# Linear attention between two FP4 feed-forwards: scores in tiles of 32 feature rows, and issued ahead of the numerator

## The chip, the core and the metric

The kernel runs on one core of a Trainium2 chip. The metric is the device time of one execution in microseconds, the median of the runs shown. A core has TensorE (matmuls; PE in the profile, PEld for its weight loads), VectorE (DVE), ScalarE (ACT), GpSimd (POOL) and SyncE (SP), which here only issues DMAs. Each engine goes through its own instructions in order; semaphores tie the engines together. Matmul results go to PSUM, eight banks of 2 KB for each of 128 partitions.

## The reference

The input x is 16 x 1024 tokens of 256 features. Three layers, each after a layernorm and with a residual:

```python
x = x + 0.5 * ffn(layernorm(x))
x = x + attention(layernorm(x))
x = x + 0.5 * ffn(layernorm(x))
# attention, 16 heads of 16 features:
q = (elu(q) + 1 + 1e-4) / 4 ; k = elu(k) + 1 + 1e-4
num[l] = q[l] @ cumsum_l(k[l] v[l]^T) ; den[l] = q[l] . cumsum_l(k[l]) + 1e-4
out = layernorm((num / den) @ Wout.T + bout) * gamma + beta
```

The feed-forward (256 to 704 to 256) rounds activations and weights to FP4 values by blocks of 16.

## The kernel before

The 16384 tokens are 128 tiles of 128 tokens; x stays in SBUF (`x_sb`). Three stages follow each other: the first feed-forward over all tiles (to about 760 us), attention (to about 1490), the second feed-forward. At the borders their steps alternate. Each stage is a software pipeline. Each engine has a step function (`sync_step`, `vector_step`, ...) that is called for i = 0, 1, 2, ... (in hardware loops of 4 steps in attention) and works on several tiles, i + 4 to i - 4; the order of the calls to it written out in the function is the order of the engine's queue, and nothing reorders it. Buffers alternate by the parity of the tile (`pair`).

Attention step i on TensorE, in order: q and k projection of tile i + 1 (L1260), transpose of k(i) (L1267), v projection of i + 1 (L1276); ten waits; numerator of i - 1, a part from the masked scores (64 matmuls, L1300) and a part from the running state (16 matmuls, L1305); scores of i (32 matmuls, L1313); the state's increments from tile i (L1328); output projection of i - 2 (L1337, L1340). A tile is split into two halves of 64 tokens. The state of the earlier tiles and halves is added through q_feat; inside a half the scores k.q are masked causally. A matmul over feature rows would add up several heads, so heads are kept apart by zeros: k is written twice (`k_eo`: rows of even heads, rows of odd heads), and q twice (`q_rows`: every other pair of heads), so that a 64 x 64 tile holds two pairs and gives 128 columns.

VectorE in step i: statistics of x(i + 4) (L1052) and of the output (L1058), the causal mask on the scores of i - 1 (L1062), residual of i - 4 (L1072), aggregates (L1074, L1076), the state `before` (L1082), gamma (L1086), the denominators of i - 1 (L1090), features of i + 1 (L1094), the reciprocal (L1097), o(i - 1) (L1103), the state's two parts (L1108, L1115).

ScalarE: high half of o(i - 2) (L1187), q_feat (L1192), q_rows (two activations, L1194), then for i + 1 the feature ramp (L1206), v (L1213), exp (L1215); k in token rows (L1223), v's own half (two, L1229), x normalized (L1235) and its high half (L1239).

GpSimd: k's even part (L1143) and odd part (L1144), low half of o(i - 2) (L1148), the state `mid` (L1155), low half of x(i + 2) (L1159), rstd (L1170, L1172), shift (L1176), beta (L1178).

SyncE: two copies of v(i + 1) to the other half (L1027), the transpose of o(i - 1) (L1033), the transpose of x(i + 3) (L1039). They wait for `v_nat`, `o_split` and `x_split`.

PSUM banks in attention: q/k 0, transpose of k and first state part 1, scores 2 and 3, v and second state part 4, numerator 5 and 6, output 7. The scores have one buffer, the numerator too.

Of the kernel before, what the change touches and what calls it, by code (L numbers as in the profile page):

```python
# [28 lines left out]
BF16 = mybir.dt.bfloat16  # L29
# [7 lines left out]
P = 128  # L37
D = 256
# [301 lines left out]
def prepare_ffn(nc, sem, scratch, wg, wu, wd, wgu_hi, wgu_lo, wd_hi, wd_lo, unscale, ident, ident16, minus_half, eps, minus_one, offsets):  # L340
# [6 lines left out]
    with ExitStack() as scope:  # L347
# [155 lines left out]
        def tensor_gate_up(pe):  # L503
            for s, (w, n, src, _) in enumerate(sets):
# [8 lines left out]
                for j, a in enumerate(src):  # L513
                    last = nc.tensor.transpose(ps[:, s % 3, j * P:(j + 1) * P], a, ident16[:])
# [27 lines left out]
        def from_bank(s):  # L542
            return ps[:, s % 3, 0:len(sets[s][2]) * P].rearrange("p (t c j) -> p c t j", c=DC, j=SUB)
# [46 lines left out]
def ffn(nc, S, T, at, N, half, x_sb, x_t, out_t, wgu_hi, wgu_lo, wd_hi, wd_lo, unscale, minus_half, eps, minus_one, offsets,  # L590
# [4 lines left out]
    with ExitStack() as scope:  # L595
# [198 lines left out]
        def scalar_step(act, i, par):  # L794
# [52 lines left out]
        def tensor_step(pe, i, par):  # L847
            tg, td = i, i - 4
            if valid(tg, N):

                if half == 1 and isinstance(tg, int) and tg == 0:
                    pe.wait_ge(T["kv_first"], N)
                    pe.wait_ge(T["o_ready"], N)
# [10 lines left out]
            if valid(td, N):  # L864
# [14 lines left out]
             "q_feat", "q_rows", "v_done", "v_nat", "v_own", "v_eo_even", "v_eo_odd", "kT_done", "k_nat", "scores_done", "masked", "kv_done", "kv_first", "kv_second",  # L879
# [8 lines left out]
class Constants:  # L888
# [11 lines left out]
    of_pair: object  # L900
    of_pair_eps: object
# [8 lines left out]
def attention_constants(sbuf, N):  # L910
    def sb(name, shape, dt=F32):
# [4 lines left out]
                     sb("of_pair", [P, 2]), sb("of_pair_eps", [P, 2]), sb("eps2", [P, 2]), sb("own", [P, DC, PAIRS]), sb("ones3", [P, P], BF16), sb("bout3", [P, D], BF16),  # L916
# [4 lines left out]
               "k_eo": (15104, 17152), "scores": 19200, "v_nat": (23296, 24384), "v_eo": (25472, 27648), "q_feat": (29824, 30848), "q_rows": (31872, 33920),  # L921
# [5 lines left out]
def attention(nc, S, at, N, x_sb, A, ident, minus_half, eps, F, attn_added, set_up):  # L927
    unscale, o_scale, one, rows, causal, diag, even, odd, of_pair, of_pair_eps, eps2, own, ones3, bout3, feat_eps, keep = (
        A.unscale, A.o_scale, A.one, A.rows, A.causal, A.diag, A.even, A.odd, A.of_pair, A.of_pair_eps, A.eps2, A.own, A.ones3, A.bout3, A.feat_eps, A.keep)
    with ExitStack() as scope:  # L930
# [19 lines left out]
        q_rows = pair("q_rows", [P, DC, 2, P])  # L950
# [5 lines left out]
        scores = sb("scores", [P, 2, DC, 2, 2, SUB])  # L956
# [38 lines left out]
        num = ps_num[:, :, 0:WIDE].rearrange("p g (h w) -> p g h w", w=VW)  # L995
# [558 lines left out]
```

## Time and profile before

| | |
|---|---|
| median of 3 runs | 2227.42 us (2226.64 to 2227.62) |
| profiled execution, its own time | 2225.92 us |
| its span, first to last instruction | 2224.2 us |
| mean granted TensorE clock | 0.994 of full speed |
| TensorE, VectorE, ScalarE, GpSimd busy | 95%, 93%, 86%, 85% |
| HBM traffic over the span | 17 GB/s |

The span is that of one execution recorded by the profiler. Busy leaves out waiting, branches and issuing of DMAs. Matmuls overlap, so a group of short ones is better read by the distance of their starts than by their durations. "issue" as the cause of idle time means that the profile shows no other instruction that the engine waited for; SPq is SyncE's queue, and a row of it is the time that issuing took, not the transfer's.

### The profile page before, as it was taken

Reading aid. Unit: us, or ns where it says so; the run is one execution under the profiler, and the core shown is the slowest. Engines: PE = TensorE matmul, PEld = TensorE weight load, DVE = VectorE, ACT = ScalarE, POOL = GpSimd, SP = SyncE. Lnnn points to the kernel's source line nnn. Section 1 sums busy time; section 2 is a strip of 40 time slices with the busy share of each in tenths; the row PEclk is TensorE's granted clock in tenths of the full one; section 3 lists DMA queues with packets and bytes.
Section 4 is the critical chain, followed back from the end, with each engine's and each line's share of the span. In section 5 each row is a group of like instructions: output and inputs, shape, how many; then the busy total and the mean of one; then the engine's idle time right before and its main releaser. Section 6 shows DMA issues by size and latency. Waiting matters only on the chain.

```text
span 2224.2 us, 91039 instructions
## 1 busy us (share of the span) xinstructions
PE 2124.0 (95%) x30384; PEld 1496.2 (67%) x30384; DVE 2066.5 (93%) x5231; ACT 1915.0 (86%) x4136; POOL 1897.5 (85%) x3002
## 2 busy tenths in 40 slices
PE   3899999999999899999999999979999999999998
PEld 1566666666666688888888888855666665666565
DVE  7999999999999689999999999978999999999997
ACT  7888888888888789999999999978888888888885
POOL 6899999999999678888888888868989999989996
PEclk9999999999999999999999999999999999999999
DMA  4765555555556432222222222224655555555555
GB/s 104 128 121 115 116 113 112 115 116 114 114 112 109 75 56 60 60 59 59 59 59 58 60 59 58 60 47 79 114 112 112 112 112 112 112 112 113 112 117 117
DMA packets 719856, 208.74 MB, mean 94 GB/s; under 512 B 666400, under 2 KB 719520, under 8 KB 719776
## 3 DMA queue, kind: packets, MB, share of 16 engines
q1 hardware_dynamic: 719776, 207.76, 46.5%
q8 instruction: 40, 0.66, 0.1%
q14 instruction: 40, 0.33, 0.1%
HBM read 20.38 MB, written 16.78 MB: 17 GB/s over the span
## 4 chain that ended last, share of the span: by engine, by line
DVE 41%; PE 25%; issue 13%; POOL 12%; DMA 4%; DVEq 2%; SPq 2%; ACT 1%; POOLq 0%; ACTq 0%
DVE ffn_y L748 10%; DVE ffn_per_block L717 9%; DVE ffn_hx L710 7%; PE ffn_ps_gu L860 6%; PE attn_ps_qk L1260 5%; DVE ffn_q L744 3%; PE ffn_ps_down L872 3%; DMA attn_xT<-attn_x_hl 3%; POOL ffn_h_hl L791 3%; POOL ffn_h_hl L790 3%; PE attn_ps_num L1300 3%; PE attn_ps_v_second L1276 2%; PE attn_ps_sc L1313 2%; DVE ffn_scale L723 2%; SPq L1033 2%
## 5 line engine op out<-in xcount | busy, mean ns | idle before, releaser
L860 PE MATMUL ffn_ps_gu<-wgu_hi,ffn_xT 128*128 128x512 f16 (+1 forms) x3072 | 739.0, 363 | 16.2 <-DVE ffn_hx L710 7.5
L860 PEld LDWEIGHTS ffn_ps_gu<-wgu_hi,ffn_xT 128*128 128x128 f16 x3072 | 300.9, 98 | 302.6 <-issue 21.7
L806 ACT ACTIVATE ffn_quarter<-ffn_y,offsets 128x960 int16<-128x960 f32 (+2 forms) x264 | 282.6, 1071 | 185.2 <-DVE ffn_y L748 185.2
L860 PE MATMUL ffn_ps_gu<-wgu_lo,ffn_xT 128*128 128x512 f16 (+1 forms) x1536 | 431.5, 363 | 0.0
L872 PE MATMUL ffn_ps_down<-wd_hi,ffn_hT 128*128 128x256 f16 x2816 | 349.9, 273 | 18.8 <-DVE x_sb L737 12.7
L790 POOL TENSOR_TENSOR ffn_h_hl<-ffn_q,ffn_h_scale_hi 128x704 f16<-128x704 f16 x256 | 352.2, 1376 | 12.5 <-DVE ffn_h_scale_lo L754 8.5
L791 POOL TENSOR_TENSOR ffn_h_hl<-ffn_q,ffn_h_scale_lo 128x704 f16<-128x704 f16 x256 | 354.0, 1383 | 0.0
L872 PEld LDWEIGHTS ffn_ps_down<-wd_hi,ffn_hT 128*128 128x128 f16 x2816 | 265.1, 98 | 99.0 <-issue 35.5
L717 DVE TENSOR_REDUCE ffn_per_block<-ffn_hx 128x60 f32<-128x960 f32 (+2 forms) x264 | 298.4, 1130 | 21.3
L748 DVE TENSOR_TENSOR ffn_y<-ffn_hx,ffn_per_block 128x960 f32<-128x960 f32 (+2 forms) x264 | 294.8, 1117 | 0.0
L842 ACT ACTIVATE ffn_odd<-ffn_quarter,offsets 128x960 f16<-128x960 int16 (+2 forms) x264 | 278.7, 1056 | 10.8 <-POOL ffn_shift L783 10.8
L710 DVE SCALAR_TENSOR_TENSOR ffn_hx<-ffn_ps_gu,unscale,ffn_silu 128x704 f32<-128x704 f32 x256 | 243.3, 950 | 13.8 <-issue 9.5
L860 PEld LDWEIGHTS ffn_ps_gu<-wgu_lo,ffn_xT 128*128 128x128 f16 x1536 | 150.8, 98 | 155.9 <-issue 3.4
L801 ACT ACTIVATE ffn_silu<-ffn_ps_gu,unscale 128x704 f32<-128x704 f32 x256 | 212.0, 828 | 17.8 <-PE ffn_ps_gu L860 17.7
L781 POOL TENSOR_TENSOR ffn_x_hl<-ffn_q,ffn_x_scale_hi 128x256 f16<-128x256 f16 x256 | 157.8, 616 | 73.5 <-POOL ffn_rstd L773 37.4
L872 PE MATMUL ffn_ps_down<-wd_lo,ffn_hT 128*128 128x256 f16 x1536 | 210.2, 273 | 0.0
L1260 PE MATMUL attn_ps_qk<-attn_xT,attn_w_hi 128*128 128x128 f16 x2048 | 179.9, 220 | 11.1 <-DMA attn_xT<-attn_x_hl 5.6
L773 POOL TENSOR_TENSOR ffn_rstd<-ffn_rstd,minus_half 128x1 f32<-128x1 f32 x256 | 167.4, 654 | 20.0
L785 POOL TENSOR_TENSOR ffn_x_hl<-ffn_q,ffn_x_scale_lo 128x256 f16<-128x256 f16 x256 | 159.9, 624 | 20.0
L872 PEld LDWEIGHTS ffn_ps_down<-wd_lo,ffn_hT 128*128 128x128 f16 x1536 | 150.6, 98 | 17.7
L1260 PEld LDWEIGHTS attn_ps_qk<-attn_xT,attn_w_hi 128*128 128x128 f16 x2048 | 135.7, 98 | 30.9 <-DMA attn_xT<-attn_x_hl 29.4
L1062 DVE TENSOR_TENSOR attn_scores<-attn_ps_sc,attn_causal 128x1024 f32<-128x1024 f32 x128 | 154.3, 1206 | 0.0
(184 smaller groups left out, 5177.6 us busy)
## 6 DMA issues: line engine op xcount, KB each, us to landing
x_sb<-in_L_attn_x SPq DMA_DIRECT2D x128, 128.0 KB, 2.4
out<-x_sb SPq DMA_DIRECT2D x128, 128.0 KB, 2.1
attn_v_eo<-attn_v_nat SPq DMA_DIRECT2D x256, 34.0 KB, 1.8
ffn_xT<-ffn_x_hl SPq DMA_TRANSPOSE x256, 2.4
ffn_hT<-ffn_h_hl SPq DMA_TRANSPOSE x256, 3.5
attn_xT<-attn_x_hl SPq DMA_TRANSPOSE x128, 2.4
attn_oT<-attn_o_hl SPq DMA_TRANSPOSE x128, 2.5
x_sb<-in_L_ffn_w_gate SPq DMA_DIRECT2D x2, 352.0 KB, 5.2
```

The costliest lines, as they stand in the source:

```text
L710: nc.vector.scalar_tensor_tensor(hx[par][:, 0:INNER], ps_gu[par][:, INNER:2 * INNER], unscale[:, 1:2], silu[:], ALU.mult, ALU.mult).then_i ...
L717: nc.vector.tensor_reduce(amax[:, blocks_in(front)], blocks(hx[par][:, front]), AXX, ALU.max, apply_absolute_value=True).then_inc(S["amax" ...
L748: nc.vector.tensor_tensor(blocks(y[:, front]), blocks(hx[par][:, front]), over_block(inv[:, at], at.stop - at.start), ALU.mult).then_inc(S ...
L773: nc.gpsimd.tensor_tensor(rstd[oth][:], rstd[oth][:], minus_half[:, 0:1], ALU.pow).then_inc(S["rstd"], 1)
L790: nc.gpsimd.tensor_tensor(blocks(h_hl[par][:, 0:INNER]), blocks(q[par][:, 0:INNER]), over_block(h_scale_hi[par][:], HB), ALU.mult)
L791: nc.gpsimd.tensor_tensor(blocks(h_hl[par][:, INNER:]), blocks(q[par][:, 0:INNER]), over_block(h_scale_lo[par][:], HB), ALU.mult).then_inc ...
L801: nc.scalar.activation(silu[:], ps_gu[par][:, 0:INNER], ACT.Silu, scale=unscale[:, 0:1]).then_inc(S["silu"], 1)
L806: nc.scalar.activation(quarter[:, back], y[:, back], ACT.Identity, bias=offsets[:, 0:1], scale=4.0 / HALF_MIN).then_inc(S["quarter"], 1)
L842: nc.scalar.activation(odd[:, back], quarter[:, back], ACT.Identity, bias=offsets[:, 1:2], scale=HALF_MIN / 4.0).then_inc(S["odd"], 1)
L860: last = nc.tensor.matmul(ps_gu[par][:, a:b], xT[par][:, c, :], w[:, k, a:b], start=(n == 0), stop=(n == len(terms) - 1))
L872: last = nc.tensor.matmul(ps_down[:, 0:D], hT[par][:, c, :], w[:, c, :], start=(n == 0), stop=(n == len(terms) - 1))
L1260: last = nc.tensor.matmul(ps_qk[:, col, :], w[:, col, k], aT, start=(n == 0), stop=(n == len(terms) - 1))
```

## The change

- Scores: instead of 32 matmuls with 64 feature rows and 128 columns (both pairs of heads through `q_rows`), 64 matmuls with 32 feature rows (one pair) and 64 columns, straight from `q_feat`. `q_rows` is gone, with its constants. Each of the four row groups writes to a bank of its own.
- PSUM: `ps_sc_num` has four banks, 2 to 5; the scores lie in columns 0 to 255 of each, the numerator in columns 256 to 391 of the last two. v and the second state part move to bank 6. The first feed-forward's `per_block` moves between its two `ps_gu`, and the set-up's transposes move by one bank.
- k's odd part moves from GpSimd to ScalarE, behind q_feat, as an activation with scale `odd` and bias `odd * 1e-4`.
- Order: on TensorE the scores of i now come after the v projection and ahead of the numerator of i - 1, with waits of their own (both parts of k, q_feat, the mask of i - 1, o of i - 2); the waits of the numerator stand behind them. On VectorE the mask of tile i moves from step i + 1 to the end of step i, and waits also for the numerator of i - 1.
- At the border to the second feed-forward its first gate/up matmuls wait for the last mask, and the second ones for the last o.

The diff, cut to this (left out: the same shift of a bank in the set-up's transposes, the lists of semaphores and constants, and `k_odd`/`q_rows` in their declarations):

```diff
@@ -626,8 +626,8 @@
         hT = pair("hT", [P, HLC, P], F16)
 
         if half == 0:
-            ps_gu = [psum(f"ps_gu{j}", [P, 3 * 512]) for j in range(2)]
-            per_block = psum("per_block", [P, 2, 256])
+            ps_gu_even, per_block, ps_gu_odd = psum("ps_gu0", [P, 3 * 512]), psum("per_block", [P, 2, 256]), psum("ps_gu1", [P, 3 * 512])
+            ps_gu = [ps_gu_even, ps_gu_odd]
             ps_down = psum("ps_down", [P, 512])
         else:
             per_block = psum("per_block", [P, 2, 256])
...
@@ -831,6 +831,7 @@
 
                 if half == 1 and isinstance(tn, int) and tn < 2:
                     act.wait_ge(T["v_done"], N)
+                    act.wait_ge(T["k_even"], N + tn - 1)
                     act.wait_ge(T["k_odd"], N + tn - 1)
                 ready(act, "shift", tn)
                 round_freed(act, "y", i + 1, 2)
...
@@ -850,6 +851,8 @@
 
                 if half == 1 and isinstance(tg, int) and tg == 0:
                     pe.wait_ge(T["kv_first"], N)
+                    pe.wait_ge(T["masked"], N)
+                if half == 1 and isinstance(tg, int) and tg == 1:
                     pe.wait_ge(T["o_ready"], N)
                 turned(pe, "xT", tg, par)
                 freed(pe, "silu", tg, 2)
...
@@ -967,9 +968,8 @@
 
         ps_qk = psum("ps_qk", [P, 2 * DC, P])
         ps_kT_first = psum("ps_kT_first", [P, 512])
-        ps_sc = psum("ps_sc", [P, 2, DC, 2, 2, SUB])
+        ps_sc_num = psum("ps_sc_num", [P, PAIRS, 512])
         ps_v_second = psum("ps_v_second", [P, 512])
-        ps_num = psum("ps_num", [P, 2, 512])
         ps_z = psum("ps_z", [P, 512])
 
         def ready(eng, name, t, k=1, per=1):
...
@@ -992,7 +992,8 @@
 
         ps_kT, ps_v = ps_kT_first[:, 0:D], ps_v_second[:, 0:D]
         WIDE = DC * PAIRS * VW
-        num = ps_num[:, :, 0:WIDE].rearrange("p g (h w) -> p g h w", w=VW)
+        ps_sc = ps_sc_num[:, :, 0:DC * P].rearrange("p r (c s q) -> p r c s q", c=DC, s=2)
+        num = ps_sc_num[:, 2:4, DC * P:DC * P + WIDE].rearrange("p g (h w) -> p g h w", w=VW)
 
         def half_state(s):
             return (ps_kT_first, ps_v_second)[s][:, D:D + WIDE]
...
@@ -1056,11 +1057,6 @@
                 if not (isinstance(tz, int) and tz < 2):
                     dve.wait_ge(S["rstd"], tz + 5)
                 nc.vector.bn_stats(z_bn6[:], ps_z[:, 0:D]).then_inc(S["z_sums"], 1)
-            if valid(tm, N):
-
-                ready(dve, "scores_done", tm)
-                nc.vector.tensor_tensor(scores[:].rearrange("p g c s j q -> p (g c s j) q"), ps_sc[:].rearrange("p g c s j q -> p (g c s j) q"),
-                                        causal[:].unsqueeze(1).to_broadcast([P, 4 * PAIRS, SUB]), ALU.mult).then_inc(S["masked"], 1)
             if valid(tz, N):
                 ready(dve, "z_sums", tz)
             if valid(ts, N):
...
@@ -1113,6 +1109,13 @@
                 if isinstance(i, int) and i == 0:
                     last_turned(dve, "hT_even")
                 nc.vector.tensor_tensor(by_head(first[:]), half_state(0).rearrange("p (h w) -> p h w", w=VW), own_head(), ALU.mult).then_inc(S["kv_first"], 1)
+            if valid(i, N):
+
+                ready(dve, "scores_done", i)
+                if valid(tm, N):
+                    ready(dve, "num_done", tm)
+                nc.vector.tensor_tensor(scores[:].rearrange("p r c s q -> p r (c s) q"), ps_sc.rearrange("p r c s q -> p r (c s) q"),
+                                        causal[:].unsqueeze(1).unsqueeze(1).to_broadcast([P, PAIRS, 2 * DC, SUB]), ALU.mult).then_inc(S["masked"], 1)
 
 
         def gpsimd_step(pool, i, par):
...
@@ -1141,7 +1144,6 @@
                 pool.sem_inc(S["turn"], 1)
                 k = expo[par][:, DC:2 * DC, :].rearrange("p c (s t) -> p c s t", s=2)
                 nc.gpsimd.tensor_scalar(k_eo[par][:, :, :, 0, :], k, FEAT_EPS, even[:], ALU.add, ALU.mult).then_inc(S["k_even"], 1)
-                nc.gpsimd.tensor_scalar(k_eo[par][:, :, :, 1, :], k, FEAT_EPS, odd[:], ALU.add, ALU.mult).then_inc(S["k_odd"], 1)
             if valid(to, N):
 
                 ready(pool, "o_hi", to)
...
@@ -1190,9 +1192,7 @@
                 ready(act, "feat", i)
                 freed(act, "num_done", i, 2)
                 nc.scalar.activation(q_feat[par][:], expo[par][:, 0:DC, :], ACT.Identity, bias=feat_eps[:]).then_inc(S["q_feat"], 1)
-                for j in range(2):
-                    last = nc.scalar.activation(q_rows[par][:, :, j, :], expo[par][:, 0:DC, :], ACT.Identity, bias=of_pair_eps[:, j:j + 1], scale=of_pair[:, j:j + 1])
-                last.then_inc(S["q_rows"], 1)
+                nc.scalar.activation(k_eo[par][:, :, :, 1, :], expo[par][:, DC:2 * DC, :].rearrange("p c (s t) -> p c s t", s=2), ACT.Identity, bias=odd_eps[:], scale=odd[:]).then_inc(S["k_odd"], 1)
             if valid(tf, N):
 
                 if isinstance(tf, int) and tf == 0:
...
@@ -1200,7 +1200,7 @@
                     act.wait_ge(F["q"], N + X_AHEAD)
                 ready(act, "qk_done", tf)
                 freed(act, "q_feat", tf, 2)
-                freed(act, "q_rows", tf, 2)
+                freed(act, "k_even", tf, 2)
                 freed(act, "k_odd", tf, 2)
                 freed(act, "kT_done", tf, 2)
                 nc.scalar.activation(expo[oth][:], ps_qk[:], ACT.Relu, bias=one[:], scale=unscale[:, 1:2]).then_inc(S["relu"], 1)
...
@@ -1275,10 +1275,25 @@
                 for n, (aT, w, k) in enumerate(terms):
                     last = nc.tensor.matmul(ps_v.rearrange("p (t m) -> p t m", t=DC), aT, w[:, 2 * DC:QT, k], start=(n == 0), stop=(n == len(terms) - 1))
                 last.then_inc(S["v_done"], 1)
+            if valid(i, N):
+
+                if isinstance(i, int) and i == 0:
+                    pe.wait_ge(F["y"], N + X_AHEAD)
+                ready(pe, "k_even", i)
+                ready(pe, "k_odd", i)
+                ready(pe, "q_feat", i)
+                freed(pe, "masked", i, 1)
+                freed(pe, "o_ready", tn, 1)
+                pe.sem_inc(S["turn"], 1)
+                for c in range(DC):
+                    for s in range(2):
+                        for a in range(2):
+                            for r in range(PAIRS):
+                                rows_of = slice(r * 2 * E, (r + 1) * 2 * E)
+                                last = nc.tensor.matmul(ps_sc[half(a), r, c, s], k_eo[par][rows_of, c, s, a], q_feat[par][rows_of, c, half(s)], start=True, stop=True)
+                last.then_inc(S["scores_done"], 1)
             if valid(tn, N):
 
-                if isinstance(tn, int) and tn == 0:
-                    pe.wait_ge(F["y"], N + X_AHEAD)
                 ready(pe, "mid", tn)
                 if not (isinstance(tn, int) and tn == 0):
                     pe.wait_ge(S["before"], tn)
...
@@ -1287,17 +1302,12 @@
                 ready(pe, "v_own", tn)
                 ready(pe, "masked", tn)
                 freed(pe, "o_ready", tn, 1)
-            if valid(i, N):
-                ready(pe, "k_odd", i)
-                ready(pe, "q_rows", i)
-                freed(pe, "masked", i, 1)
-            if valid(tn, N):
                 for c in range(DC):
                     for r in range(PAIRS):
                         for u in range(4):
                             s, m = u // 2, u % 2
                             h = c * PAIRS + r % 2 * 2
-                            nc.tensor.matmul(num[quarter(u), r // 2, h:h + 2, :], scores[:, r // 2, c, s, r % 2, quarter(m)], v_eo[oth][:, s, :, c * PAIRS + r, :],
+                            nc.tensor.matmul(num[quarter(u), r // 2, h:h + 2, :], scores[:, r, c, s, quarter(m)], v_eo[oth][:, s, :, c * PAIRS + r, :],
                                              start=(c == 0 and r % 2 == 0), stop=False, skip_group_check=True)
                 for c in range(DC):
                     for s, st in enumerate((before, mid)):
...
@@ -1305,13 +1315,6 @@
                             last = nc.tensor.matmul(num[half(s), g, c * PAIRS:(c + 1) * PAIRS, :], q_feat[oth][half(g), c, half(s)], st[oth][half(g), c],
                                                     start=False, stop=True, skip_group_check=True)
                 last.then_inc(S["num_done"], 1)
-            if valid(i, N):
-                for c in range(DC):
-                    for s in range(2):
-                        for a in range(2):
-                            for g in range(2):
-                                last = nc.tensor.matmul(ps_sc[half(a), g, c, s], k_eo[par][half(g), c, s, a], q_rows[par][half(g), c, :, half(s)], start=True, stop=True)
-                last.then_inc(S["scores_done"], 1)
             if valid(i, N):
 
                 ready(pe, "k_nat", i)
...
@@ -1464,9 +1465,7 @@
         last.then_inc(top_ready, 1)
         dve.wait_ge(even_ready, 1)
         nc.vector.tensor_scalar(A.odd[:], A.even[:], -1.0, 1.0, ALU.mult, ALU.add).then_inc(done, 1)
-        dve.wait_ge(pair_ready, 1)
-        then(dve, nc.vector.tensor_tensor(of_pair[:], in_pair[:, 0:2], in_pair[:, 2:4], ALU.add))
-        nc.vector.tensor_scalar(A.of_pair_eps[:], of_pair[:], FEAT_EPS, None, ALU.mult).then_inc(done, 1)
+        nc.vector.tensor_scalar(A.odd_eps[:], A.even[:], -FEAT_EPS, FEAT_EPS, ALU.mult, ALU.add).then_inc(done, 1)
 
     def tops_made(pe):
         pe.wait_ge(top_ready, 1)
```

## Rows read from the trace of the kernel before

**Rows 1.** The page's busy time per engine, share of the span, instructions.
```profile
PE 2124.0 (95%) x30384; PEld 1496.2 (67%) x30384; DVE 2066.5 (93%) x5231; ACT 1915.0 (86%) x4136; POOL 1897.5 (85%) x3002
```

**Rows 2.** Windows, attention stage: length, busy time by engine, clock, DMA share, GB/s.
```profile
760.00:1460.00 700.00, 680.22 (x20567) 599.20 (x20561) 650.31 (x1714) 651.65 (x1479) 562.20 (x1105) 1.00 0.30 59
```

**Rows 3.** Source line L1090, 820 to 1440 us: duration, first and last start, waits.
```profile
L1090 DVE TENSOR_SCALAR attn_den<-attn_ps_num,attn_o_scale x110: 233/234/236, 824.7 to 1436.0; 128x16 f32<-128x16 f32 x110
...
  PE attn_ps_num L1305: 25.7, 92
```

**Rows 4.** Waits, 900 to 1300 us: who waited for whom, total, times, longest.
```profile
PEld attn_ps_num L1300 <- issue: 22.2, 71, 0.5
...
PEld attn_ps_qk L1260 <- DMA attn_xT<-attn_x_hl: 11.3, 39, 0.4
...
PE attn_ps_num L1300 <- issue: 5.6, 26, 0.2
```

**Rows 5.** Timeline 1116 to 1122 us: start, length, instruction, idle before it.
```profile
1116.29 0.23 DVE L1090 TENSOR_SCALAR attn_den<-attn_ps_num,attn_o_scale 128x16 f32<-128x16 f32 x1 [0.37 <-PE attn_ps_num L1305]
...
1117.38 0.42 DVE L1103 TENSOR_TENSOR attn_o<-attn_ps_num,attn_rden 128x256 f32<-128x256 f32 x1
...
1118.19 0.42 DVE L1052 BATCH_NORM_STATS2 attn_bn<-x_sb 128x6 f32 x1
...
1116.35 0.64 ACT L1229 ACTIVATE attn_v_eo<-attn_v_nat 64x136 f32<-64x136 f32 x2 [0.23 <-PE attn_ps_num L1305]
...
1117.98 0.40 ACT L1187 ACTIVATE attn_o_hl<-attn_o 128x256 f16<-128x256 f32 x1
...
1118.25 0.48 POOL L1144 TENSOR_SCALAR attn_k_eo<-attn_expo,attn_odd 128x256 f32<-128x256 f32 x1
1118.81 0.67 POOL L1148 TENSOR_TENSOR attn_o_hl<-attn_o,attn_o_hl 128x256 f16<-128x256 f32 x1
...
1119.71 1.19 SPq L1033 DMA_TRANSPOSE attn_oT<-attn_o_hl  x1
1121.16 1.19 SPq L1039 DMA_TRANSPOSE attn_xT<-attn_x_hl  x1
```

**Rows 6.** The same view, 1125 to 1133 us: the way from the transpose to the denominators.
```profile
1125.97 0.76 PE L1300 MATMUL attn_ps_num<-attn_v_eo,attn_scores 128*32 128x34 f32 x64
...
1126.66 0.28 PE L1305 MATMUL attn_ps_num<-attn_before,attn_q_feat 64*64 64x68 f32 x2
...
1126.80 1.19 SPq L1039 DMA_TRANSPOSE attn_xT<-attn_x_hl  x1
...
1126.95 1.05 PE L1313 MATMUL attn_ps_sc<-attn_q_rows,attn_k_eo 64*64 64x128 f32 x32
...
1129.29 0.40 PE L1260 MATMUL attn_ps_qk<-attn_xT,attn_w_hi 128*128 128x128 f16 x4
...
1131.62 0.90 PE L1300 MATMUL attn_ps_num<-attn_v_eo,attn_scores 128*32 128x34 f32 x64
1132.44 0.28 PE L1305 MATMUL attn_ps_num<-attn_before,attn_q_feat 64*64 64x68 f32 x2
...
1132.98 0.23 DVE L1090 TENSOR_SCALAR attn_den<-attn_ps_num,attn_o_scale 128x16 f32<-128x16 f32 x1 [0.34 <-PE attn_ps_num L1305]
```

**Rows 7.** Groups by line and shape, 900 to 1300 us: busy, mean ns, idle before.
```profile
L1062 DVE TENSOR_TENSOR attn_scores<-attn_ps_sc,attn_causal 128x1024 f32<-128x1024 f32 x72 | 86.8, 1206 | 0.0
...
L1194 ACT ACTIVATE attn_q_rows<-attn_expo,attn_of_pair_eps,attn_of_pair 128x256 f32<-128x256 f32 x144 | 77.6, 586 | 0.0
...
L1313 PE MATMUL attn_ps_sc<-attn_q_rows,attn_k_eo 64*64 64x128 f32 x2272 | 75.1, 269 | 0.0
...
L1300 PE MATMUL attn_ps_num<-attn_v_eo,attn_scores 128*32 128x34 f32 x4544 | 58.5, 198 | 5.7 <-issue 5.6
...
L1192 ACT ACTIVATE attn_q_feat<-attn_expo,attn_feat_eps 128x256 f32<-128x256 f32 x72 | 35.5, 493 | 0.0
...
L1144 POOL TENSOR_SCALAR attn_k_eo<-attn_expo,attn_odd 128x256 f32<-128x256 f32 x71 | 34.0, 478 | 6.6
```

More of the change, by code:

```diff
@@ L513, in tensor_gate_up @@
                 for j, a in enumerate(src):
-                    last = nc.tensor.transpose(ps[:, s % 3, j * P:(j + 1) * P], a, ident16[:])
+                    last = nc.tensor.transpose(ps[:, 1 + s % 3, j * P:(j + 1) * P], a, ident16[:])
                 last.then_inc(set_turned, 1)
@@ L878 @@
 ATTN_SEMS = ("sums", "stats", "var", "rstd", "shift", "xn", "x_hi", "x_split", "turn", "xT_even", "xT_odd", "qk_done", "relu", "exp", "feat", "k_even", "k_odd",
-             "q_feat", "q_rows", "v_done", "v_nat", "v_own", "v_eo_even", "v_eo_odd", "kT_done", "k_nat", "scores_done", "masked", "kv_done", "kv_first", "kv_second",
+             "q_feat", "v_done", "v_nat", "v_own", "v_eo_even", "v_eo_odd", "kT_done", "k_nat", "scores_done", "masked", "kv_done", "kv_first", "kv_second",
              "mid", "before", "num_done", "den", "rden", "o_ready", "o_hi", "o_split", "oT_even", "oT_odd", "proj_done",
@@ L915, in attention_constants @@
                      sb("rows", [P, 3, D]), sb("causal", [P, SUB]), sb("diag", [P, DC, 2 * PAIRS]), sb("even", [P, 1]), sb("odd", [P, 1]),
-                     sb("of_pair", [P, 2]), sb("of_pair_eps", [P, 2]), sb("eps2", [P, 2]), sb("own", [P, DC, PAIRS]), sb("ones3", [P, P], BF16), sb("bout3", [P, D], BF16),
+                     sb("odd_eps", [P, 1]), sb("eps2", [P, 2]), sb("own", [P, DC, PAIRS]), sb("ones3", [P, P], BF16), sb("bout3", [P, D], BF16),
                      sb("feat_eps", [P, 1]), sb("keep", [P, N]))
 ATTN_PLACES = {"o": 8352, "oT": (1024, 2048), "o_hl": (9376, 4096), "mid": (5632, 6176), "before": (6720, 7264), "first": 7808, "second": 11264, "k_nat": 12352, "zg": 13376,
-               "k_eo": (15104, 17152), "scores": 19200, "v_nat": (23296, 24384), "v_eo": (25472, 27648), "q_feat": (29824, 30848), "q_rows": (31872, 33920),
+               "k_eo": (15104, 17152), "scores": 19200, "v_nat": (23296, 24384), "v_eo": (25472, 27648), "q_feat": (29824, 30848),
                "expo": (35968, 38016), "xT": (40064, 41088), "x_hl": (42112, 43136), "xn": 44160,
@@ L927, in attention @@
 def attention(nc, S, at, N, x_sb, A, ident, minus_half, eps, F, attn_added, set_up):
-    unscale, o_scale, one, rows, causal, diag, even, odd, of_pair, of_pair_eps, eps2, own, ones3, bout3, feat_eps, keep = (
-        A.unscale, A.o_scale, A.one, A.rows, A.causal, A.diag, A.even, A.odd, A.of_pair, A.of_pair_eps, A.eps2, A.own, A.ones3, A.bout3, A.feat_eps, A.keep)
+    unscale, o_scale, one, rows, causal, diag, even, odd, odd_eps, eps2, own, ones3, bout3, feat_eps, keep = (
+        A.unscale, A.o_scale, A.one, A.rows, A.causal, A.diag, A.even, A.odd, A.odd_eps, A.eps2, A.own, A.ones3, A.bout3, A.feat_eps, A.keep)
     with ExitStack() as scope:
@@ L955, in attention @@
         v_eo = pair("v_eo", [P, 2, 2, HEADS // 2, VW])
[L956 removed]
+        scores = sb("scores", [P, PAIRS, DC, 2, SUB])
         first, second = sb("first", [P, DC, PAIRS, VW]), sb("second", [P, DC, PAIRS, VW])
```

12 lines of the change are left out of this document (4 added, 8 removed).

## The prediction, made before the changed kernel was run

> **What bounds the kernel now.** I read the page's busy shares first, then the stage that the change touches, then the waits inside it, then single steps in order of time. Over the span TensorE and VectorE are busy 95% and 93% [rows 1], which names no bound. In the attention stage TensorE, VectorE and ScalarE stand at 97%, 93% and 93% and GpSimd at 80%, at full granted clock [rows 2]. L1090 (the denominators, once a step) starts 110 times between 824.7 and 1436.0 us [rows 3]: (1436.0 - 824.7) / 109 = 5.608 us a step. That is the number the change must move.
>
> No engine is full, so I look for loops: chains that come back to the same instruction some steps later and so set the step. VectorE waits for the numerator on TensorE before L1090 in 92 of 110 steps, 25.7 us in all. TensorE waits for the transposed x (DMA) ahead of the q/k projection in 39 of 71 steps, 11.3 us [rows 3, 4]. Both point to one way round: numerator(k) on TensorE, denominators and o(k) on VectorE, the high half of o on ScalarE (L1187), the low half on GpSimd (L1148), SyncE's transpose of o (L1033), then SyncE's transpose of x(k+4) behind it (L1039), the q/k projection(k+4) and, later in that same TensorE step, numerator(k+2). From k to k+2: two steps.
>
> Its first part in the trace [rows 5]: L1090 at 1116.29, o_hi ends at 1118.38, but o_lo starts only at 1118.81 since GpSimd was still on k's odd part until 1118.73; transpose of o at 1119.71, of x at 1121.16. Its second part [rows 6]: transpose of x at 1126.80, q/k projection at 1129.29 (2.49 later), numerator at 1131.62 (2.33), its second half L1305 at 1132.44 (0.82; in another step 1125.97 to 1126.66, 0.69), L1090 at 1132.98 (0.54). So from projection to denominators 2.33 + 0.75 + 0.54 = 3.62, and the way round is (1121.16 - 1116.29) + 2.49 + 3.62 = 10.98 over two steps, 5.49 a step. That is 0.12 under 5.608. The rest belongs to a three-step variant, in which GpSimd reaches o_lo late for its own reasons (rstd, shift, beta, k's two parts): the three steps from 1116.29 to 1132.98 are 16.69, 5.56 each.
>
> **The change, part by part.**
>
> *ScalarE* loses the two q_rows copies (2 x 586 ns, back to back 1.08) and gains one 128x256 activation like L1192, 493 ns [rows 7]: 0.6 to 0.7 us less a step. They stand behind L1187 in its order, so they never delayed o_hi of their step; what they delayed was the next L1229. That one also waits for the numerator: at 1116.35, released by the numerator like L1090, it starts 0.06 after it, and the chain to o_hi's end is 1118.38 - 1116.29 = 2.09 [rows 5]. I use 2.09, the case in which ScalarE is not late.
>
> *GpSimd* loses L1144, 478 ns [rows 7] and with its gap 1118.81 - 1118.25 = 0.56 [rows 5]. That is the stall that goes. What is late next is o_hi: o_lo can't start before 2.09 plus a hand-over. The trace has no such hand-over in the open; the nearest are numerator to ScalarE, 0.06, and o_lo's end (1119.48) to SyncE, 0.23 [rows 5]. I take 0.15. So o_lo starts 2.24 after L1090 instead of 2.52, a gain of 0.28, not 0.56. New first part: 2.24 + 0.67 + 0.23 to the transpose of o, + 1.45 to the transpose of x (SyncE spends 1.19 on the first) = 4.59, + 2.49 = 7.08.
>
> *TensorE, scores.* 32 matmuls of 64x64, 128 columns, become 64 of 32 rows, 64 columns. The old ones start 26.7 ns apart at best (1132.73 on; 32 take 0.87 with the change of shape) [rows 6]. The new ones are as many as L1300's, whose 64 take 0.69 to 0.82 including the hand-over to L1305, some 11 to 13 ns each. Bounds: if eight small ones run where four large ones ran, each costs 26.7 / 4 = 6.7 ns, 0.43 in all; if still only four run at a time, 26.7 / 2 = 13.3 ns, 0.85. I take 0.75, nearest to L1300. On TensorE's own account this is a gain of about 0.1. The Trainium skill (TensorEngine Tiling, Available Configurations) lists 32x64 as eight independent tiles; by that the 0.43 would hold and my forecast would fall by 0.16 a step, but the trace's L1300 doesn't reach such a pace.
>
> *TensorE, order.* This is the part that costs. Before, the scores of step i came behind numerator(i-1), while VectorE, ScalarE, GpSimd and SyncE were already on the way back; they were off the loop. Now they stand between the v projection and the numerator, so all of their 0.75 is added between projection and denominators. In front of the scores: waits for k_even, k_odd, q_feat, masked, o_ready and a semaphore increment, fewer than the ten that stood ahead of the numerator. Behind them: seven waits ahead of the numerator, now right after 64 short matmuls, where TensorE has no backlog to hide them. Bounds: 0, and the weight load's 22.2 / 71 = 0.31 of idle "issue" ahead of L1300 [rows 4]; TensorE itself idled only 5.6 / 71 = 0.08 there. I take 0.10. New second part: 3.62 + 0.75 + 0.10 = 4.47.
>
> What comes behind the numerator (state matmuls, out projection) follows it directly now. It needs k_nat and the transpose of o; no row shows how much they have to spare. I take them as in time, since ScalarE is relieved and the transpose of o is issued 4.59 - 1.45 = 3.14 after L1090 and lands in the 2.49 of a transpose, 5.63, while the projection comes a step and some tenths later.
>
> *VectorE.* The masking, 1206 ns for 1024 elements [rows 7], stays the same size and moves from behind the two bn_stats to behind L1115. That makes a one-step loop: masked(i), scores(i+1), numerator(i), L1090, ..., L1115, masked(i+1). L1115 ends its turn at 1118.19, 1.90 after L1090 [rows 5]; + 1.21, a hand-over 0.15 to 0.3, + 0.85, + 0.75 + 0.54 = 5.40 to 5.55. It is under the two-step loop, so masked isn't what TensorE waits for, but it isn't far away.
>
> *Shared banks.* Scores and numerator share two banks, in different columns; masked(i) waits for numerator(i-1), scores(i) for o(i-2). In program order both are long done. Nothing.
>
> *Set-up and the feed-forward stages:* a few tiny set-up operations go, the banks of the first feed-forward are renumbered, the last masking comes some time earlier. I cost them at nothing, cover being the loads at the start; bound 1 to 2 us either way.
>
> **The sum.** Two-step loop (7.08 + 4.47) / 2 = 5.775 a step. Three-step loop 16.69 - 0.56 + 0.85 = 16.98, 5.66 a step, not the bound. One-step loop at most 5.55. So the step goes from 5.608 to 5.775, +0.167. It counts for 109 full steps and, at about half, for the 18 that run beside feed-forward steps: 118 x 0.167 = +19.7. The profiled execution took 2225.9 us for a span of 2224.2; its own sum is 2245.6, and the median of the runs shown is 1.5 above it, so 2246 to 2247. I say 2246.
>
> Own range of this case: shortest 7.00 + 3.56 + 0.43, 5.50, where the other loops hold the step at about 5.55 to 5.6, no change; longest 7.16 + 3.69 + 0.85 + 0.31 = 12.01, 6.00 a step, +0.40 x 118 = +47, 2273.
>
> **Rivals.**
>
> *A. The relief wins: faster.* Mechanism: place GpSimd and ScalarE between L1090 and the transpose of o. For it: three engines stand at 93% or more, and a three-step loop through GpSimd is as tight as the trace gets; if that way back, not TensorE's stretch, sets the step, it loses 0.56 on GpSimd and 0.68 on ScalarE against 0.85 added: 16.69 - 1.24 + 0.85 = 16.30, 5.43 a step, -0.17 x 118 = -20, 2206. It decides once o_hi's end lies more than 0.5 earlier than 2.09 after L1090. Against it: q_rows stand behind o_hi, and ScalarE then waits for the numerator anyway.
>
> *B. It nets out.* Scores at the pace of eight tiles and waits hidden: 5.6 a step, 2223 to 2232.
>
> *C. The small score matmuls are no cheaper each than the large ones* (26.7 ns, 64 of them 1.71). Then the second part is 3.62 + 1.71 + 0.10 = 5.43, (7.08 + 5.43) / 2 = 6.25 a step, +76, 2302. Against it: L1300's 64 matmuls go at 11 to 13 ns each. The Trainium skill (TensorE: Matmul & The Clock Gate, "Wait — 56ns, not 53.3ns?") says that starts never come closer than about 25 ns however small the matmul; by that rule this case would be the result, but the same row contradicts it.
>
> **Chances.** Forecast 0.64, A 0.18, B 0.10, C 0.08. The range 2220 to 2276 leaves out nearly all of A below (0.12) and C above. The likeliest case's own range is 2228 to 2273. A measurement of this kernel tells a change from none at about 0.2%, 4.5 us: slower 0.68 (nearly all of the forecast, C), same 0.13 (B and the forecast's low end), faster 0.19 (A).
>
> **What would show it.** In the trace after: L1090's step near 5.78 in the same stretch; TensorE busy share falling by some 3 points, with nearly every step idle ahead of the q/k projection, put down to the transpose of x; score matmuls taking 0.7 to 0.8 from first start to the numerator's first; projection to denominators 4.4 to 4.6 instead of 3.6; o_lo starting right behind o_hi, 2.2 to 2.3 after L1090, with GpSimd idle ahead of it; ScalarE's busy share down to some 80% (5.22 busy of 5.608 now, less 0.66, over 5.775). Wrong it would be if TensorE doesn't wait for x at all (then A), or if it waits for masked ahead of the scores (then the one-step loop is longer than I made it), or if the scores take 1.5 or more (C).

## The result and the profile after

The changed kernel takes 2257.6 us (2256.1 to 2260.1), beside 2227.0 for the kernel before: ratio 1.014, interval 1.012 to 1.016. It is slower, by 30.6 us; the forecast was 19 slower, 2246, inside the range but too low. The profiled execution took 2260.1 us for a span of 2258.4.

The attention stage in windows (columns as in [rows 2]):

```profile
760.00:1460.00 700.00, 671.74 (x23729) 577.98 (x23724) 597.25 (x1661) 579.30 (x1311) 482.85 (x950) 1.00 0.27 57
```

The denominators' line, now L1086, in the stretch of [rows 3]:

```profile
L1086 DVE TENSOR_SCALAR attn_den<-attn_ps_sc_num,attn_o_scale x107: 232/234/236, 823.9 to 1435.1; 128x16 f32<-128x16 f32 x107
...
  PE attn_ps_sc_num L1315: 60.6, 107
```

The same line over the whole run:

```profile
L1086 DVE TENSOR_SCALAR attn_den<-attn_ps_sc_num,attn_o_scale x128: 226/234/236, 767.2 to 1524.0; 128x16 f32<-128x16 f32 x128
```

A step takes (1435.1 - 823.9) / 106 = 5.766 us against 5.608: +0.158, and VectorE now waits for the numerator in every step (92 of 110 in [rows 3]). On 109 steps that is +17.2. But from the first to the last denominators it is 756.8 us against 723.9 (the same line of the kernel before starts at 767.3 first and at 1491.2 last), +32.9. So 15.7 us were lost in the 18 steps at the borders, where attention alternates with a feed-forward. The two profiled executions are 34.2 us apart, so all but 1.3 us lies in attention. Relieved engines gave nothing back: ScalarE went from 652 to 579 busy and GpSimd from 562 to 483, in 700 us. VectorE, which lost no work, fell from 650 to 597 all the same: there are fewer steps in the stretch, and its residual takes 485 ns instead of 782 (means from 900 to 1300 us); no run tests why.

The waits, 900 to 1300 us (who waited for whom, total us, times, longest):

```profile
ACT attn_v_eo L1229 <- PE attn_ps_sc_num L1315: 49.4, 69, 0.8
...
DVE attn_den L1086 <- PE attn_ps_sc_num L1315: 38.3, 69, 0.8
POOL attn_o_hl L1150 <- ACT attn_o_hl L1189: 35.1, 70, 0.6
...
PEld attn_ps_qk L1260 <- DMA attn_xT<-attn_x_hl: 16.6, 36, 0.5
...
PE attn_ps_qk L1260 <- DMA attn_xT<-attn_x_hl: 5.7, 28, 0.3
```

The engines wait for one another along the way round: ScalarE and VectorE for the numerator, GpSimd for o's high half, TensorE's loads for the transpose of x. One turn of the loop in the timeline (start, length, instruction, idle before it):

```profile
1112.16 0.23 DVE L1086 TENSOR_SCALAR attn_den<-attn_ps_sc_num,attn_o_scale 128x16 f32<-128x16 f32 x1 [0.73 <-PE attn_ps_sc_num L1315]
...
1113.92 0.40 ACT L1189 ACTIVATE attn_o_hl<-attn_o 128x256 f16<-128x256 f32 x1
...
1114.41 0.68 POOL L1150 TENSOR_TENSOR attn_o_hl<-attn_o,attn_o_hl 128x256 f16<-128x256 f32 x1 [0.64 <-ACT attn_o_hl L1189]
...
1115.24 1.19 SPq L1034 DMA_TRANSPOSE attn_oT<-attn_o_hl  x1
1116.70 1.19 SPq L1040 DMA_TRANSPOSE attn_xT<-attn_x_hl  x1
...
1119.10 0.40 PE L1260 MATMUL attn_ps_qk<-attn_xT,attn_w_hi 128*128 128x128 f16 x4 [0.17 <-DMA attn_xT<-attn_x_hl]
...
1121.42 0.91 PE L1293 MATMUL attn_ps_sc_num<-attn_q_feat,attn_k_eo 32*64 32x64 f32 x64
1122.42 0.76 PE L1310 MATMUL attn_ps_sc_num<-attn_v_eo,attn_scores 128*32 128x34 f32 x64
...
1123.64 0.23 DVE L1086 TENSOR_SCALAR attn_den<-attn_ps_sc_num,attn_o_scale 128x16 f32<-128x16 f32 x1 [0.67 <-PE attn_ps_sc_num L1315]
```

First part 1119.10 - 1112.16 = 6.94, second 1123.64 - 1119.10 = 4.54, together 11.48 for two steps, 5.74 (means from 1000 us on: 6.99 and 4.55). The step alternates between some 5.6 and 5.9, and the wait for x comes about once in the two steps.

### The profile page after: what moved, and what is told of

It is laid out like the page before. It is cut to its first block and busy times, and to the rows that moved or that the text cites. A ratio compares the mean times of both kernels' runs of the same rounds, so it can differ in the third digit from the quotient of the medians.

```text
span 2258.4 us, 99286 instructions
## 1 busy us (share of the span) xinstructions
PE 2144.9 (95%) x34480; PEld 1498.4 (66%) x34480; DVE 2029.6 (90%) x5229; ACT 1861.4 (82%) x4008; POOL 1832.7 (81%) x2874
## 5 line engine op out<-in xcount | busy, mean ns | idle before, releaser
L1229 ACT ACTIVATE attn_v_eo<-attn_v_nat 64x136 f32<-64x136 f32 x256 | 80.5, 315 | 104.8 <-PE attn_ps_sc_num L1315 103.3
L875 PEld LDWEIGHTS ffn_ps_down<-wd_lo,ffn_hT 128*128 128x128 f16 x1536 | 150.6, 98 | 17.7
```

The source lines that it names most:

```text
L875: last = nc.tensor.matmul(ps_down[:, 0:D], hT[par][:, c, :], w[:, c, :], start=(n == 0), stop=(n == len(terms) - 1))
```

## The borders

In the straight-line code there, TensorE stops in the middle of blocks that hold no wait. An example (timeline, TensorE):

```profile
1483.11 0.61 PE L1310 MATMUL attn_ps_sc_num<-attn_v_eo,attn_scores 128*32 128x34 f32 x47
1485.75 0.34 PE L1310 MATMUL attn_ps_sc_num<-attn_v_eo,attn_scores 128*32 128x34 f32 x17 [2.04 <-issue]
```

47 of 64 matmuls, 2.04 us of nothing, then the other 17. In the stretches 730 to 860 and 1400 to 1530 us I count stops of TensorE of 0.8 us or more that end by "issue" in attention's own blocks: 2 in the kernel before (1.85, 0.95; 2.8 together), 9 in the changed one (1.54, 1.09, 1.75, 2.20, 1.85, 2.04, 2.14, 2.13, 2.06; 16.8 together). From 830 to 1440 us, inside the hardware loop, there is none. The DMA queue for instructions, from the page of the changed kernel (packets, MB); it was 40 packets and 0.66 MB before:

```profile
q8 instruction: 44, 0.72, 0.1%
```

That is four packets of 16 KB more; between 900 and 1300 us that queue moves nothing. The times of its packets in the traces tie the stops to it. In each of the nine stops of the changed kernel TensorE goes on 1.31 to 1.51 us after the last such packet has landed. For the stop shown, the packet starts at 1483.50 and lands at 1484.44, and TensorE goes on at 1485.75. In the two stops of the kernel before it is 1.35 and 1.33. So in the straight-line code TensorE stops for instructions that come in by DMA while it runs.

The stops grew by 14.0 us, but that isn't simply the loss of 15.7. From the first to the 13th denominators and over the last 13 steps, where all the stops lie, the two kernels take 151.7 and 168.7 us. Of these 17.0 us (4.0 of them are the longer loop, 25 x 0.158) TensorE's idle time makes 8.9 and its busy time 8.1. The stops replaced other waits: waits of 0.8 us or more for another engine or a transpose fell from 8.1 to 3.6 us in these steps. And the busy time grew by more than the 2.5 that 25 steps of the loop would add (5.51 busy a step before, 5.61 after). The last 13 steps, before and after, columns as in [rows 2]:

```profile
1413.50:1491.20 77.70, 68.10 (x2110) 59.41 (x2102) 67.22 (x176) 66.32 (x158) 58.21 (x118) 0.99 0.30 54
...
1435.10:1524.00 88.90, 74.93 (x2461) 62.72 (x2461) 64.06 (x175) 60.71 (x145) 50.61 (x103) 0.88 0.26 47
```

The granted clock was 0.88 there instead of 0.99: some 20 us at the lower level, 1.2 GHz, instead of 2. It falls at 1471.0, 1494.9 and 1508.6 us, each time near the end of a stop of about 2 us. At that level the same blocks take longer:

```profile
1510.42 1.06 PE L1343 MATMUL attn_ps_z<-attn_w_hi,attn_oT 128*128 128x256 f16 x4
...
1513.51 1.27 PE L1293 MATMUL attn_ps_sc_num<-attn_q_feat,attn_k_eo 32*64 32x64 f32 x64 [0.86 <-ACT attn_k_eo L1195]
```

In the loop they take 0.60 and 0.91. Over the whole of an execution the granted clock is 0.988 or 0.989 in all four of the changed kernel, and 0.991 to 0.995 in all those of the kernel before. No run separates what the stops cost from what the lower clock costs. The experiments had to say whether the number of instructions makes the stops or the new order.

## The experiments

The step of each kernel is read as above, from its line of the denominators between 820 and 1440 us. Ratios are to the kernel before in the same rounds.

**order_alone**: the old 32 score matmuls, q_rows and k's odd part on GpSimd stay; only the order is new.

```diff
-            (moved from here: scores behind the numerator; mask behind the two bn_stats)
+                ready(pe, "k_odd", i)
+                ready(pe, "q_rows", i)
+                freed(pe, "masked", i, 1)
+                pe.sem_inc(S["turn"], 1)
+                (the 32 score matmuls, then the numerator's waits; mask(i) at the end of VectorE's step)
```

> The kernel before with one part of the change: the scores (the old 32 matmuls of 64x64, q_rows and k's odd part on GpSimd kept) issued ahead of the numerator, and the mask at the end of VectorE's step. Theory (two-step loop, with the scores now inside it): the first part stays as before, 4.87 + 2.49, the second becomes 3.62 + 0.87 + 0.10 = 4.59, together 11.95, so about 5.95 a step against 5.61, +0.34 on 118 steps, some 2268 us. Rival 1 (not this loop sets the step, but TensorE's total or the mask's one-step loop): 5.6 to 5.65 a step, 2228 to 2234. For the borders between the stages: if the stops of 1 to 2.2 us in the middle of TensorE's blocks after the change come from the number of its instructions in straight-line code, there are as few here as before (one or two); if they come from the order, there are eight or nine.

Measured 2269.2 us, ratio 1.021 (1.019 to 1.022).

```profile
L1085 DVE TENSOR_SCALAR attn_den<-attn_ps_num,attn_o_scale x105: 232/234/236, 822.8 to 1436.4; 128x16 f32<-128x16 f32 x105
```

(1436.4 - 822.8) / 104 = 5.90 a step, 5.95 expected: +0.29. The order alone costs more than the whole change: the rest of the change takes back 0.13 a step. From the scores' first matmul to the numerator's first it is 1.03 us here and 0.95 in the changed kernel, so the small tiles give 0.08 of the 0.27 on the loop of two steps; the rest isn't shown part by part. Rival 1 is out. At the borders it has 5 stops, 8.1 us together: fewer than the changed kernel, more than the one or two expected. Each ends 1.31 to 1.47 us after an instruction packet has landed.

Its first part did not stay as before: the transpose of x starts 4.60 after the denominators, not 4.96 as in the kernel before (4.56 in the changed kernel; means from 1000 us on). k's odd part is still on GpSimd here, yet o's low half starts at 2.27 instead of 2.63.

**scores_in_64**: the kernel before with twice as many score matmuls, of half the columns.

```diff
-    last = nc.tensor.matmul(ps_sc[half(a), g, c, s], k_eo[par][half(g), c, s, a], q_rows[par][half(g), c, :, half(s)], ...)
+    for j in range(2):
+        last = nc.tensor.matmul(ps_sc[half(a), g, c, s, j], k_eo[par][half(g), c, s, a], q_rows[par][half(g), c, j, half(s)], ...)
```

> The kernel before, with each score matmul of 128 columns issued as two of 64 columns, same tiles, same place, same results. The scores stay outside the loop and the array's work is the same (2 x 13.3 ns for 26.7), so every theory of the loop expects 5.61 a step, at most 5.65. Theory of the borders (TensorE's straight-line code is fetched too slowly once a step has 32 matmuls more and short ones): stops of about 2 us in the middle of blocks, some 5 to 9 of them, +8 to +14 us, 2236 to 2241. Rival (the stops come from the new order): none more than before, 2227 to 2229.

Measured 2255.1 us, ratio 1.014 (1.012 to 1.015): more than expected, for two reasons. The borders have 10 stops, 17.3 us together, in the old order, and the instruction queue has 44 packets as in the changed kernel (40 in order_alone); each stop ends 1.26 to 1.48 us after one has landed. So the number of TensorE's instructions makes most of them. All thirteen kernels bear it out: those with 32 score matmuls have 1 to 5 such stops, those with 64 have 7 to 11. And the step grew to (1434.4 - 827.5) / 106 = 5.725, which I had excluded. Its scores and the state's first matmul in the timeline:

```profile
1119.32 1.26 PE L1314 MATMUL attn_ps_sc<-attn_q_rows,attn_k_eo 64*64 64x64 f32 x64
1120.45 0.24 PE L1329 MATMUL attn_ps_kT_first<-attn_v_nat,attn_k_nat 64*64 64x68 f32 x1
```

64 take 1120.45 - 1119.32 = 1.13, 17.7 ns each, where half of 26.7 would be 13.3 and the block 0.85. Off the loop, 0.2 to 0.25 more of TensorE's time still cost 0.12 a step. From 820 to 1440 us TensorE is busy 616.8 of 620 us here, and 608.9 in the kernel before, which leaves it 0.10 idle a step. So in the kernel before TensorE's own work is itself close to the step.

**after_x_first** and **before_x_first**: x ahead of o on SyncE and GpSimd.

```diff
+    (sync_step)   if valid(tx, N): ... dma_start_transpose(xT ...)      # now ahead of oT
     (sync_step)   if valid(to, N): ... dma_start_transpose(oT ...)
+    (gpsimd_step) if valid(tx, N): ... x_hl low half                    # now ahead of o's
     (gpsimd_step) if valid(to, N): ... o_hl low half
```

> The changed kernel, with the transpose of x issued ahead of that of o on SyncE, and x's low half ahead of o's low half on GpSimd. That cuts the two-step loop: x no longer waits for o. Theory: the next bounds hold, numerator to denominators to features to the next projection, 4.55 + 0.89 + 0.1 = 5.54, and the mask's one-step loop, 5.55; so 5.55 to 5.6 a step instead of 5.77, and 2232 to 2238 us. Rival (the one-step loop through the mask, or the seven new waits, set the step and the wait for x was only the last to end): 5.72 to 5.77 a step, 2252 to 2258.

> The kernel before, with the same swap (x ahead of o on SyncE and GpSimd). Theory: TensorE's wait for x goes and the step falls to what TensorE and ScalarE have of their own, 5.45 to 5.55 instead of 5.61, so -0.06 to -0.16 on 118 steps: 2208 to 2220 us. Rival (three engines at 93% and more set the step together, the loop through SyncE only fills what is left): 5.6 a step, 2225 to 2229.

Both wrong, and in sign: 2286.0 us (ratio 1.029, 1.027 to 1.030) and 2248.3 us (1.011, 1.010 to 1.013). The step went to (1436.5 - 822.7) / 102 = 6.02 and (1437.8 - 825.4) / 106 = 5.78. What TensorE waited for ahead of the output projection in after_x_first, 820 to 1440 us (its wait and its loads' together):

```profile
  DMA attn_oT<-attn_o_hl: 82.0, 106
```

The transpose of o is needed too, one block earlier in TensorE's order than that of x. Put behind x on SyncE and GpSimd, it starts 4.20 us after the denominators instead of 3.10 and lands late, and the output projection holds up the q/k projection behind it: the same two-step loop with another transpose at its end. I had given o a slack that it doesn't have.

**after_o_hi_first** and **before_o_hi_first**: o's high half between x normalized and x's high half on ScalarE; in the kernel before also o's low half ahead of k's odd part.

```diff
+            if valid(to, N):                      # to = i - 1 now
+                ready(act, "o_ready", to)
+                nc.scalar.activation(o_hl[oth][:, 0:D], o[:], ACT.Copy).then_inc(S["o_hi"], 1)
             if valid(tn, N):
                 ready(act, "xn", tn)
```

> The changed kernel, with o's high half ahead of x's high half on ScalarE. Theory (two-step loop): the high half is held by o itself then and ends some 2.0 us after the denominators instead of 2.15; 0.15 off a loop of two steps, -0.07 a step, 5.70 instead of 5.77, and 2247 to 2251 us. Rival (the step is set by TensorE's own blocks or by the mask): 5.77, no change.

> The kernel before, with o's high half ahead of x's high half on ScalarE, and o's low half between k's even and odd part on GpSimd (so 0.3 and 0.5 us earlier); SyncE's order is kept. Theory (two- and three-step loops set the step together with TensorE's own 5.45 to 5.5): the transpose of o starts 0.5 earlier, that of x is then held by x's low half, 0.3 earlier; 5.50 to 5.57 a step instead of 5.61, so 2211 to 2221 us. Rival (TensorE's and ScalarE's own work set the step, the wait for x fills what is left): 5.6 a step, no change.

Changed kernel: 2253.0 us, ratio 1.012 (1.010 to 1.013), step (1435.5 - 824.0) / 107 = 5.715, so 0.05 less for a transpose of o that starts 0.14 earlier (2.96 after the denominators instead of 3.10, mean of the steps from 1000 us on). Half of 0.14 would be 0.07. Kernel before: 2226.6, ratio 0.9999 (0.999 to 1.001). Its transpose of o started 2.96 instead of 3.50 after the denominators. But the transpose of x, which ends the loop, started only 0.12 earlier (4.84 instead of 4.96), and TensorE, at the q/k projection 0.08 earlier, began the numerator 0.06 later (4.39 instead of 4.33). So this run hardly shortened the loop through x. It shows that the way to o's transpose alone doesn't hold the step; what the loop through x is worth there it can't tell.

**after_odd_on_gpsimd**: k's odd part back from ScalarE.

```diff
-    nc.scalar.activation(k_eo[par][:, :, :, 1, :], ..., ACT.Identity, bias=odd_eps[:], scale=odd[:]).then_inc(S["k_odd"], 1)
+    nc.gpsimd.tensor_scalar(k_eo[par][:, :, :, 1, :], k, FEAT_EPS, odd[:], ALU.add, ALU.mult).then_inc(S["k_odd"], 1)
```

> The changed kernel, with k's odd part back on GpSimd. Theory (two-step loop): o's low half starts at 2.38 after the denominators instead of 2.23, since GpSimd is still on the odd part; +0.15 on the loop of two steps, +0.07 a step, 5.84, and 2262 to 2267 us. Rival 1 (GpSimd's relief was worth all of its 0.56 over two or three steps): 5.95 to 6.05, 2280 and more. Rival 2 (ScalarE, relieved by 0.6, is what counts): 5.7 or less, faster than the changed kernel.

Measured 2261.1 us, ratio 1.015 (1.014 to 1.017), step (1437.6 - 825.0) / 106 = 5.779. That is 0.01 over the changed kernel where 0.07 was expected, and its ratio can't be told from 1.014. Both rivals are out: GpSimd's 0.56 was worth next to nothing here, ScalarE's added activation costs nothing. The trace shows why it is less than 0.07. The transposes start 0.11 later (3.21 and 4.67 after the denominators, not 3.10 and 4.56), but from the q/k projection to the numerator it takes 0.05 less (3.28 instead of 3.33). That would leave 0.03 a step; the last 0.02 stays open.

**after_fewer_waits**: three waits ahead of the numerator gone.

```diff
-                ready(pe, "q_feat", tn)
-                ready(pe, "masked", tn)
-                freed(pe, "o_ready", tn, 1)
```

> The changed kernel without the three waits ahead of the numerator that the scores' waits already cover (q_feat, masked and o_ready of the tile before). The distance from the first score matmul to the numerator's first is 0.96 us. If waits right behind 64 short matmuls cost TensorE some 0.03 to 0.05 each, it falls to 0.82 to 0.87, and half of that counts: 5.70 to 5.72 a step, 2249 to 2252 us. If the drain at the change of tile shape hides them, nothing changes: 0.96, 5.77, 2257.

Measured 2253.0 us, ratio 1.012 (1.010 to 1.013), step (1434.8 - 823.8) / 107 = 5.710. From the scores' first matmul to the numerator's it is 0.87 instead of 0.95 (means from 1000 us on). So a wait behind a block of short matmuls costs some 30 ns (an estimate, 0.08 over three waits), and about half of it counts.

**after_both**: the last two edits of the changed kernel together.

> The changed kernel with o's high half earlier and without the three covered waits, the two edits that took 0.05 and 0.06 a step each. Both lie on the two-step loop, so they add up if it holds the step: 5.65 to 5.67 a step, 2245 to 2248 us. If another loop (the mask's one-step loop, features to the next projection) lies close below: 5.70, 2251 to 2253.

Measured 2246.2 us, ratio 1.009 (1.008 to 1.011).

```profile
L1086 DVE TENSOR_SCALAR attn_den<-attn_ps_sc_num,attn_o_scale x110: 232/233/236, 820.3 to 1436.3; 128x16 f32<-128x16 f32 x110
```

(1436.3 - 820.3) / 109 = 5.651: -0.051 and -0.056 alone, -0.115 together. Two edits at different places of the way round each gave about half of what they took off it, and they add up: with order_alone this shows the two-step loop as the bound of the changed kernel. It also shows what is left: this step is 0.04 over the old one, some 5 us, and the kernel is still 21 us slower, so the rest is the borders.

**before_mask_last** and **before_mask_last_o_hi**: in the kernel before, the wait for the mask is the last ahead of the numerator, its double gone; the second has before_o_hi_first's edits too.

```diff
                 ready(pe, "v_own", tn)
-                ready(pe, "masked", tn)
                 freed(pe, "o_ready", tn, 1)
             if valid(i, N):
                 ready(pe, "k_odd", i)
                 ready(pe, "q_rows", i)
-                freed(pe, "masked", i, 1)
             if valid(tn, N):
+                ready(pe, "masked", tn)
```

> The kernel before, with the wait for the mask as the last of the waits ahead of the numerator, and its double taken out: o_ready, k_odd and q_rows are waited for ahead of it. Moving o and x earlier didn't shorten the step of the kernel before, so a shorter loop holds it. Theory: the mask's one-step loop. The mask ends 3.81 after the denominators on average, the numerator starts at 4.32, the next denominators at 5.62; four waits lie in the 0.51. With one left the numerator starts at 4.10 to 4.20, held by the v projection then (4.20 to 4.26): 5.48 to 5.55 a step instead of 5.61, 2212 to 2220 us. Rival (TensorE's own blocks and the drain after the v projection set the step): 5.6, no change.

> The same, with o's high and low half earlier as in the run before_o_hi_first. If the mask's loop and the two-step loop are both near the step of the kernel before, neither edit alone gives all: together 5.45 to 5.50 a step (TensorE's own blocks), 2208 to 2215 us, some 3 to 6 us under before_mask_last. If only the mask's loop counts: as before_mask_last, within 2 us.

2225.2 us, ratio 1.000 (0.999 to 1.001), and 2222.7 us, ratio 0.9984 (0.9975 to 0.9993). Steps (1437.1 - 820.1) / 110 = 5.609 and (1435.3 - 821.3) / 110 = 5.582. The first alone changed nothing; the numerator still started 4.32 after the denominators (4.33 before). Only both together gain, 0.026 a step. This version is the fastest of all, 0.16% by the ratio and 2.7 us by the medians under the kernel before, far less than expected. The kernel before is held by several things at once. One is TensorE's own work, which leaves only 0.10 a step; which the others are stays open.

## Why the prediction was right, and where it was too small

*The order puts the scores inside the two-step loop: right.* 7.08 + 4.47 was forecast for the two parts and 5.775 a step; 6.99 + 4.55 on average and 5.766 came. order_alone shows that it is the order: +0.29 by itself.

*The scores' block: a little too small.* 0.75 + 0.10; measured 1.00 from their first to the numerator's first in the turn shown, 0.95 on average. 64 matmuls of 32 rows keep L1300's pace or somewhat less, neither the 6.7 ns of eight tiles at once nor the 26.7 of rival C. The Trainium skill (TensorE: Matmul & The Clock Gate, "Wait — 56ns, not 53.3ns?") states that starts never come closer than about 25 ns; by that the block would take an estimated 1.6 us. 64 in 0.91 contradict it for matmuls that go to different tiles of the array.

*GpSimd's relief: the right number, in part for a wrong reason.* The first part came out 0.09 shorter than forecast and made up for the scores, which is luck. The forecast took 0.28 off it because k's odd part leaves GpSimd. o's low half does start at 2.23 after the denominators, as forecast (2.24), and GpSimd's 35.1 us of waiting for L1189 show that o's high half holds it then. But with the odd part still on GpSimd it starts at 2.27 in order_alone and 2.34 in after_odd_on_gpsimd, against 2.63 in the kernel before. So most of the gain comes with the new order and its longer step, in which GpSimd gets to k's even part earlier after the denominators (1.14 in order_alone instead of 1.50), and the relief itself was worth 0.01 a step. ScalarE's relief is worth nothing, as forecast, as far as it was tested: taking another 0.59 off it gains nothing. One item was simply missing: k's odd part on ScalarE takes 586 ns, not 493, without effect.

*Rival A failed* because the work taken off ScalarE and GpSimd hardly shortened the way round; B because the waits and the pace of the scores weren't hidden.

*The 18 steps at the borders "at about half": this step failed.* They had 1.5 us in the sum, and 15.7 us came. I took them for the steady step at half effect. I didn't ask what 64 more TensorE instructions a step mean where the code is straight-line: a load and a matmul each for 32 more matmuls. What came in its place is nine stops for instructions instead of two, 14.0 us more of them, partly in place of other waits, and 20 instead of 2 us at the lower clock. "Set-up and the feed-forward stages at nothing" held: 17.2 + 15.7 = 32.9 of the 34.2 us between the profiled executions lie in attention, 1.3 outside it.

*"TensorE's busy share falls by some 3 points, nearly every step waits for x": wrong.* It fell from 97% to 96%, for 32 more matmuls are busy time too. TensorE's loads waited for x in 36 of 69 steps (39 of 71 before), only longer, 16.6 us instead of 11.3. A two-step loop needs only one wait in two steps.

*What bounded the kernel before: too simple.* I named the loops through SyncE. scores_in_64 lengthened TensorE's own block, off these loops, and the step grew by 0.12; before_o_hi_first brought the transpose of o forward by half a us and nothing happened, though it moved that of x by only 0.12. The forecast held all the same, since one loop was lengthened past all others.

## What to carry to other kernels

Ask of every block what waits for the end of the block behind it. An instruction group that fills time after the last thing others wait for is free; the same group ahead of that is paid for in full on the loop, divided by the steps the loop spans. More and shorter matmuls in straight-line code have a second price, the fetching of instructions, which a steady loop doesn't show: look at the borders on their own, at the times of the instruction queue's packets and at the granted clock.

## What the runs showed of the hardware

- In straight-line code TensorE stops 1 to 2.3 us at a time in the middle of blocks: 2 stops with 32 score matmuls a step, 10 with 64, in the same order. Inside the hardware loop there was none in either. In the four kernels before, after, order_alone and scores_in_64 all 26 such stops end 1.26 to 1.51 us after a 16 KB packet of the instruction queue has landed, so they are waits for instructions.
- In the last 13 attention steps of the changed kernel the granted clock fell to the lower level (1.2 GHz) near the end of stops of about 2 us, and four 128x256 matmuls took 1.06 us instead of 0.60.
- Splitting a float32 matmul of a 64x64 tile and 128 columns into two of 64 columns doesn't halve its time: 26.7 ns between starts became 17.7, not 13.3. With 32x64 tiles, 64 of them take 0.91 us.
- Two transposes issued by one queue are 1.45 us apart, and which goes first is part of the loop: the swap, together with that of GpSimd's low halves, cost 0.25 us a step in the changed kernel and 0.17 in the kernel before.
